# Three residual sums moved from VectorE adds into PSUM accumulation on TensorE, drained by ScalarE copies

## The reference

```
h = tok(x)                      # windowed attention: 8x8 windows, 8 heads of 8, 2D rotary, proj + proj_b
h = h + mamba(layernorm(h))     # RMS norm, in_proj, causal conv of 4 taps, silu, selective scan, out_proj,
                                #   + residual (its own normed input)
h = h + moe(layernorm(h))       # 6 experts of three layers, weights of the top 2 from a router
```

## Time and profile before

| | before |
|---|---|
| median of 3 runs | 1697.93 us (1687.25 to 1699.51) |
| profiled execution | 1679.58 us |
| its span, first to last instruction | 1677.8 us |
| PE busy | 1269.9 us (76%) |
| DVE busy | 1313.0 us (78%) |
| ACT busy | 1047.0 us (62%) |
| POOL busy | 1106.3 us (66%) |
| mean granted clock of TensorE | 0.877 |

### The profile page before, as it was taken

The page is one execution under the profiler, slowest core; times in us unless marked ns, Lnnn a source line. Parts: engine busy times, 40 slices in busy tenths (PEclk is TensorE's granted clock), DMA queues, the critical chain, the costliest instruction groups (busy, mean ns, idle before and its releaser), DMA issues. The chain is left out here.

```text
span 1677.8 us, 25769 instructions
## 1 busy us (share of the span) xinstructions
PE 1269.9 (76%) x7988; PEld 594.3 (35%) x7988; DVE 1313.0 (78%) x1719; ACT 1047.0 (62%) x1940; POOL 1106.3 (66%) x1523
## 2 busy tenths in 40 slices
PE   3675768797978778796979787887969696767565
PEld 2442515243433434252524333343425242121212
DVE  2122478898988898998989898988889798979951
ACT  2235566768677676867676777767685767474522
POOL 2013376877767686868687786868686877877740
PEclk9768988899999999898989999998999998676765
DMA  2000569686968686767767687868677687778820
GB/s 69 1 13 7 159 171 258 179 234 176 247 184 228 190 230 193 207 204 188 229 176 234 184 239 195 223 189 220 195 213 203 174 232 205 230 205 234 237 71 7
DMA packets 212961, 303.35 MB, mean 181 GB/s; under 512 B 77196, under 2 KB 77400, under 8 KB 212696
## 3 DMA queue, kind: packets, MB, share of 16 engines
q1 hardware_dynamic: 212824, 301.70, 65.0%
HBM read 274.75 MB, written 20.97 MB: 176 GB/s over the span
## 5 line engine op out<-in xcount | busy, mean ns | idle before, releaser
L1279 POOL TENSOR_TENSOR hc<-hs,c_rep 128x512 f32<-128x512 f32 x512 | 655.3, 1281 | 313.1 <-DVE hs L1062 311.1
L1062 DVE TENSOR_TENSOR_SCAN hs<-bank,state,xd 128x512 f32<-128x512 f32 x512 | 651.6, 1275 | 51.5 <-issue 36.0
L808 ACT ACTIVATE bank<-dl,a_neg 128x512 f32<-128x512 f32 x512 | 350.3, 686 | 165.4 <-DVE hs L1062 118.5
L1053 DVE TENSOR_TENSOR xd<-xd,bank 128x512 f32<-128x512 f32 x512 | 336.5, 662 | 27.6 <-DMA xd<-xdel_rows 22.4
L548 PE MATMUL bank<-q_diag,k_heads 128*128 128x128 f32 x1024 | 189.9, 308 | 10.1 <-ACT shift L801 10.1
L548 PEld LDWEIGHTS bank<-q_diag,k_heads 128*128 128x128 f32 x1024 | 167.1, 198 | 83.1 <-issue 77.5
L538 PE MATMUL bank<-k_heads,q_diag 128*128 128x512 f32 x256 | 160.5, 712 | 40.5 <-ACT pv L801 19.9
L816 ACT ACTIVATE probsT<-bank 128x512 f32<-128x512 f32 x128 | 76.4, 597 | 174.9 <-PE bank L549 174.9
L457 PE MATMUL bank<-hc,wts 128*32 128x512 f32 x1024 | 175.4, 744 | 5.2 <-POOL hc L1279 5.2
L1080 DVE TENSOR_REDUCE neg_max<-bank 128x8 f32<-128x512 f32 x128 | 87.9, 687 | 99.7 <-PE bank L538 99.0
L739 PE MATMUL bank<-e,wts 64*64 64x512 f32 x368 | 63.5, 764 | 78.8 <-ACT e L986 78.8
(11 more groups left out here) (162 smaller groups left out, 2207.0 us busy)
## 6 DMA issues: line engine op xcount, KB each, us to landing
xd<-xdel_rows SPq DMA_DIRECT2D x512, 256.0 KB, 4.5
dl<-delta_rows SPq DMA_DIRECT2D x512, 256.0 KB, 4.1
delta_rows<-delta SPq DMA_DIRECT2D x16, 512.0 KB, 7.6
xdel_rows<-xdel SPq DMA_DIRECT2D x16, 512.0 KB, 5.7
xin<-in_x_dram SPq DMA_DIRECT2D x32, 128.0 KB, 2.6
q_diag<-rot SPq DMA_DIRECT2D x32, 128.0 KB, 2.8
out_dram<-res SPq DMA_DIRECT2D x256, 16.0 KB
k_heads<-rot SPq DMA_DIRECT2D x104, 16.0 KB
```

What stands on the lines that cost most here:

```text
L808: act.activation(decay_ps[n % 2][:, :], dl[:, n % 4, :], ACT.Exp, scale=a_neg[:, g:g + 1])\
L1053: dve.tensor_tensor(xd[:, n % 8, :], xd[:, n % 8, :], b_ps[:, :], ALU.mult).then_inc(injected.sem, 1)
L1062: dve.tensor_tensor_scan(hs[:, n % 4, :], decay_ps[n % 2][:, :], xd[:, n % 8, :], state[:, u:u + 1], ALU.mult, ALU.add).then_inc(scanned.s ...
L1279: pool.tensor_tensor(hc[:, n % 8, :], hs[:, n % 4, :], c_rep[:, BAND * h:BAND * h + BAND], ALU.mult)\
```

## The change

Each sum is now made in PSUM. PE first multiplies the second summand by the identity (a 128x128 stationary `ident`, 512 moving columns, `start=True`), and the products that were there follow with `start=False`, so they accumulate on it. For "out" the four transposes become four plain products with the identity as the moving operand, as they too must accumulate. The three DVE adds are gone. ACT copies each finished bank to SBUF (hid, h1, res) and signals `drained`: hid in `normalize` n = 8, h1 in `experts` n = 5, res in `experts` n = 35. The reduces on DVE stay where they were. The call of `experts` for chunk c-2 leaves DVE's body, as nothing is left in it.

```diff
@@ tensor
                 if s == 31:
                     use = A["proj"]
                     fill(use, k)
+                    pe.matmul(use.bank[:, :], ident, h_bias[:, :].unsqueeze(1).to_broadcast([128, NW, C]),
+                              start=True, stop=True)
                     pe.wait_ge(A["oT"].drained, A["oT"].empty(k))
                     for i in range(4):
                         last = pe.matmul(use.bank[:, 128 * i:128 * i + 128], attT[:, 128 * i:128 * i + 128], col("wp"),
-                                         start=True, stop=True)
+                                         start=False, stop=True, skip_group_check=True)
...
                 if n == 4:
                     use = F["mo"]
                     fill(use, k)
+
+                    pe.wait_ge(ln1_pool.sem, ln1_pool.at(k, 15))
+                    pe.matmul(use.bank[:, :], ident, h_ln[:, q, :, :], start=True, stop=True)
                     pe.wait_ge(gated.sem, gated.at(k, 2))
                     for w in range(NW):
                         last = pe.matmul(use.bank[:, C * w:C * w + C], y_gated[:, w, :, :], col("w_out"),
-                                         start=True, stop=True)
+                                         start=False, stop=True, skip_group_check=True)
...
                 if n == SLOTS + 2:
                     use = F["out"]
                     fill(use, k)
+                    pe.matmul(use.bank[:, :], ident, h1[:, :, :], start=True, stop=True)
                     for i in range(4):
-                        last = pe.transpose(use.bank[:, 128 * i:128 * i + 128], outT[:, 128 * i:128 * i + 128], ident)
+                        last = pe.matmul(use.bank[:, 128 * i:128 * i + 128], outT[:, 128 * i:128 * i + 128], ident,
+                                         start=False, stop=True, skip_group_check=True)
@@ scalar
             def normalize(k, n):
+                if n == 8:
+                    use = A["proj"]
+                    act.wait_ge(use.filled, use.full(k))
+                    if past(k - 1):
+                        act.wait_ge(ln1_pool.sem, ln1_pool.at(k - 1, 15))
+                    copy(hid[:, :, :], use.bank[:, :].rearrange("p (w h) -> p w h", w=NW)).then_inc(use.drained, 1)
...
             def experts(k, n):
+                if n == 5:
+                    use = F["mo"]
+                    act.wait_ge(use.filled, use.full(k))
+                    copy(h1[:, :, :], use.bank[:, :].rearrange("p (w h) -> p w h", w=NW)).then_inc(use.drained, 1)
+                if n == SLOTS + 3:
+                    use = F["out"]
+                    act.wait_ge(use.filled, use.full(k))
+                    if past(k - 1):
+                        act.wait_ge(stored.sem, stored.at(k - 1, 256))
+                    copy(res[:, :, :], use.bank[:, :].rearrange("p (w h) -> p w h", w=NW)).then_inc(use.drained, 1)
@@ vector
-                if n == 8:
-                    use = A["proj"]
...
-                    dve.tensor_tensor(hid[:, :, :], use.bank[:, :].rearrange("p (w h) -> p w h", w=NW),
-                                      h_bias[:, :].unsqueeze(1).to_broadcast([128, NW, C]), ALU.add)\
...
-                    dve.tensor_tensor(h1[:, :, :], use.bank[:, :].rearrange("p (w h) -> p w h", w=NW), h_ln[:, q, :, :], ALU.add)\
-                       .then_inc(use.drained, 1)
                     dve.wait_ge(F["mo"].drained, F["mo"].empty(k))
                     dve.tensor_reduce(st[:, 0, :], h1[:, :, :], X_AXIS, ALU.add).then_inc(done.sem, 1)
...
-                    dve.tensor_tensor(res[:, :, :], use.bank[:, :].rearrange("p (w h) -> p w h", w=NW), h1[:, :, :],
-                                      ALU.add).then_inc(use.drained, 1)
```

More of the change, by code:

```diff
@@ L611, in second, with experts @@
                     from_x(k, q, "c1", "wc", 1)
-            def experts(k, n):
+            def experts(k, q, n):
                 if n == 4:
@@ L766, in body @@
                     if has(c - 2):
-                        experts(c - 2, SLOTS + n)
+                        experts(c - 2, odd, SLOTS + n)
                     if has(c - 1) and n == 1:
@@ L774, in body @@
                     if has(c - 1):
-                        experts(c - 1, n)
+                        experts(c - 1, 1 - odd, n)
                     if has(c + 1):
@@ L1111, in normalize @@
                 st, done = st_a, ln1_dve
-                if n == 8:
-                    use = A["proj"]
-                    dve.wait_ge(use.filled, use.full(k))
-                    if past(k - 1):
-                        dve.wait_ge(ln1_pool.sem, ln1_pool.at(k - 1, 15))
-                    dve.tensor_tensor(hid[:, :, :], use.bank[:, :].rearrange("p (w h) -> p w h", w=NW),
-                                      h_bias[:, :].unsqueeze(1).to_broadcast([128, NW, C]), ALU.add)\
-                       .then_inc(use.drained, 1)
                 if n == 9:
@@ L1133, in prepare, with experts @@
                     dve.tensor_scalar(xdel[:, :], ex_d[:, :], 1.0, -1.0, ALU.add, ALU.add).then_inc(soft_dve.sem, 1)
-            def experts(k, q, n):
+            def experts(k, n):
                 st, done = st_f, ln2_dve
                 if n == 5:
-                    use = F["mo"]
-                    dve.wait_ge(use.filled, use.full(k))
-                    dve.wait_ge(ln1_pool.sem, ln1_pool.at(k, 15))
-                    dve.tensor_tensor(h1[:, :, :], use.bank[:, :].rearrange("p (w h) -> p w h", w=NW), h_ln[:, q, :, :], ALU.add)\
-                       .then_inc(use.drained, 1)
                     dve.wait_ge(F["mo"].drained, F["mo"].empty(k))
@@ L1211, in body @@
                         gated_out(c, odd, 0)
-                    if has(c - 2):
-                        experts(c - 2, odd, SLOTS + n)
                     if has(c + 1):
@@ L1220, in body @@
                     if has(c - 1):
-                        experts(c - 1, 1 - odd, n)
+                        experts(c - 1, n)
             dve.memset(rw2_2[:, :], 0.0).then_inc(setup_dve, 1)
```

## The result

The change makes the kernel slower: 1796.0 us against 1695.2 us, the medians of four runs each, a ratio of 1.061 (95% interval 1.057 to 1.065). The forecast was 1798 us.

What follows compares the result with a forecast made beforehand. It took the chain PE, ACT, PE, ACT, not DVE's load, to pace slots 2 to 11. Twelve full passes at 7.0 us (84) plus 16 elsewhere gave +100 on the median 1697.93: 1798 us, range 1740 to 1830.

Steps and rivals of the forecast that it cites:

- the order decides, not DVE's load: Slots 2 to 11: the PE-ACT chain paces, not DVE's load; the load rival had 1668 us, chance 0.05.
- PE, slots 2 to 4: New products cost PE 1.39 us in slot 2 and 0.96 in slot 4; ACT's conv results move about 3.0 us.
- hid behind the table block: Slots 8 and 9: ACT copies hid only after table loads and Silu; DVE waits, scan 10 is 7.1 us late.
- what the hid stall leaves at the end of a pass: The wait for hid adds 2.6 us to xdel, 5.6 late in all, and later slots give nothing back.
- the clock, 1.4 us a pass in slots 9 to 12: PE's 6.3 us idle before k and q may lower the clock: 0 to 2.7 us on xdel, 1.4 taken.
- the replay: Slots 2 to 13 of pass 8 stepped through with durations as issued: xdel at 963.5 instead of 957.90, 5.6 late.
- the clock falls for longer: Rival: the 6 us gap keeps PE at 1.2 GHz into the attention slots; +116 to +136 us, chance 0.10.
- everything outside the full passes: Pass 0 3 us, pass 1 4, pass 14 3, pass 15 1.5, lead-in 2, tail 2.5: 16 us in sum.

Runs made afterwards that it cites:

- e7: The kernel before with only the sum of hid moved, ACT's copy of it placed ahead of the table loads; 1699.9 us, 1.007.
- e6: The kernel before with all of PE's added products, overwritten by those that follow, and DVE's adds kept; 1713.4 us, 1.012.
- e9: The kernel before plus the filler, one 512-column identity product on PE in slot 3 that nobody reads; 1666.8 us, 0.988.
- e4: The changed kernel with one call moved: ACT copies hid ahead of the table loads and Silu; 1754.3 us, 1.038 to the kernel before.
- e8: The changed kernel plus the filler, one 512-column identity product on PE in slot 3 that nobody reads; 1769.8 us, 1.046 to the kernel before.
- e1: The kernel before with only the sum of hid moved, as the diff has it; 1756.6 us, 1.042.
- e5: The kernel before with ACT's three copies, no DVE adds and no identity products, the second summands left out; 1783.9 us, 1.057.
- e3: The kernel before with only the sum of res (out) moved, as the diff has it; 1748.1 us, 1.038.
- e2: The kernel before with only the sum of h1 moved, as the diff has it; 1695.7 us, 1.004.
- e12: The kernel before plus the product in slot 3, with ACT's first z copy ahead of attention's copy in slot 6; 1671.7 us, 0.987.
- e10: The kernel before plus unread products on PE: one in slot 3, one at the end of slot 11, three in slot 16; 1674.6 us, 0.991.

## Why the prediction came out, step by step

**Right: the order decides, not DVE's load.** The 30 us that DVE sheds bring no gain. The Trainium skill (Perfetto Trace Analysis, Optimizing Scalar/DVE Operations) says that if DVE is saturated, offloading some work to Scalar may make sense. Here it didn't: with DVE busy for 90% of a pass, one sum moved with its copy well placed gave 1.007 (e7).

**Right: PE, slots 2 to 4.** From scan 0 the conv starts at 16.0 us in pass 9 (1099.74 - 1083.72) against 13.2 in pass 8 of before (933.58 - 920.34): 2.8 later, foretold 2.9. Scan 6 is 5.65 later (20.41 against 14.76), foretold 5.9. It is caught up to 2.5 by scan 9 (foretold 3.0). In e6's passes with the clock up scan 9 is 2.0 us later than in e9 (25.82 against 23.85 after scan 0), so most of this is PE's; the other 0.5 comes with ACT's copies.

**Right: hid behind the table block.** The copy starts as the second load ends, and scan 10 is 6.8 us later than before (33.02 against 26.21), foretold 7.1. e4 against the changed kernel shows it by one moved call. The price by the Trainium skill (ScalarE: Activation LUTs, What ACT_TABLE_LOAD costs), 2.66 us a switch, would have put hid 2.7 us later still; the rows have 1.30 us from 1110.99 to 1112.29, and 1.30 from 1114.21 to the copy, so the measurement speaks against it here.

**Mis-sized: what the hid stall leaves at the end of a pass.** xdel is 5.8 us later (43.37 after scan 0, was 37.56), as replayed; I then wrote "later slots are not touched" and let the pass carry 5.6. But the lateness changes on the way: scan 14 is 5.1 late, scan 19 is 6.2 late. In both kernels DVE then waits for a transfer of xd; before and after, pass 9:

```profile
1061.49 0.69 DVE L1053 TENSOR_TENSOR xd<-xd,bank 128x512 f32<-128x512 f32 x1 [1.22 <-DMA xd<-xdel_rows]
```

```profile
1140.70 0.69 DVE L1076 TENSOR_TENSOR xd<-xd,bank 128x512 f32<-128x512 f32 x1 [2.19 <-DMA xd<-xdel_rows]
```

SP issues it behind k_heads, which are made from POOL's rot. Timelines of SP, before, then after:

```profile
1048.04 3.02 SPq L349 DMA_DIRECT2D k_heads<-rot  x4
...
1057.45 0.60 SPq L337 DMA_DIRECT2D xd<-xdel_rows  x1
```

```profile
1127.21 3.01 SPq L349 DMA_DIRECT2D k_heads<-rot  x4
...
1136.60 0.60 SPq L337 DMA_DIRECT2D xd<-xdel_rows  x1
```

From their pass's scan 0 (1010.80 and 1083.72) these are at 37.2 and 46.7 us before, 43.5 and 52.9 after: the queue is 6.2 us late, and so are the scans once they need it. That the queue is what fixes the 6.2 is read from the rows; no run moved it alone. With the clock held in slots 2 to 8 (e8 and e9) a pass costs 6.4 us: 2.5 by scan 9 and 4.0 behind it (e1 alone has about 4 too), for which I had 2.6 for the stall and 1.4 for the clock.

**Mis-sized: the clock, 1.4 us a pass in slots 9 to 12.** It does fall to the low level in the gap, as the rows of L476 and L457 show. But I had priced the stretch as if it ran at full clock before. Over slots 10 to 13 of pass 8 of before, and of pass 9 of after, it is

```profile
946.55:959.23 12.68, 7.89 (x36) 2.28 (x29) 11.22 (x15) 11.09 (x17) 10.23 (x16) 0.81 0.71 186
```

```profile
1116.74:1127.70 10.96, 9.12 (x57) 2.31 (x50) 10.51 (x14) 7.00 (x13) 8.68 (x13) 0.87 0.54 144
```

0.81 before, 0.87 after: the low stretch only begins earlier. xdel of pass 9 is only 0.2 us later than the replay without any clock term. In e8 this stretch alternates between 10.9 us with 2.8 us at the low clock, as in pass 9, and 11.9 us with 5.0, so every second pass has 1 us more. The term is then an estimated 0.2 + 0.5 = 0.7 us on average instead of 1.4. It is contained in the 4.0, whose stall is then 3.3 rather than 2.6.

**Missed: the clock in slots 4 to 6.** The rival "the clock falls for longer" had it in the attention slots, as a consequence of the gap. It comes earlier, ahead of the gap, and one product in slot 3 removes it. It costs 3.3 us in slots 4 to 8 and 4.3 in the whole pass in passes 8, 10 and 12, and it is in the kernel before too (its passes 5, 6 and 12 take 92.0, 92.0 and 93.7 us instead of 89.8 to 91.7). The change made it more frequent: of passes 2 to 13, three have it before, six after, seven in e1, ten in e5, twelve in e3, but only three in e6 and two in e2. Why it comes in one pass and not in the next is open.

**Mis-sized: everything outside the full passes.** I had 16 us. Between e8 and e9 it is: first scan 4.9 us later (foretold 2), pass 0 9.3 (3), pass 1 4.3 (4), pass 14 3.8 (3), pass 15 -0.5 (1.5), tail 6.1 (2.5), together 28. The filler doesn't hold the clock in e8's pass 0; between the two kernels themselves pass 0 costs 2.3 and the whole sum is 24. The single traces spread here: e2 has the same program as the kernel before up to its first scan, and that comes at 202.9 us instead of 194.6. So the terms of a few us can't be told apart. For the tail I had read no row, and no run took it apart.

So 84 + 16 = 100 was 93 + 24 = 117 between the profiled executions of the two kernels, both terms too small, above all for the clock in slots 4 to 8; with the filler in both it was 77 + 28 = 105. The medians moved by 101, because the profiled execution of the kernel before (1679.58 us) lies 15.6 us under its median, while that of the changed kernel (1796.58) lies at it. Where the slower executions of the kernel before lose these 15.6 us no trace shows. The agreement to 2 us is in part luck; the mechanism isn't.

## What to carry to other kernels

Moving work from a full engine to a less busy one can pay only if the result is there by the time its readers need it. So look up what stands ahead of it in its new engine's order: here a table block of 4.5 us, and moving one call ahead of it, with the same instructions, was worth 42 us. A stall's own length says little: 4.5 us before h1 cost 0.5 us alone, since DVE could catch up, while 4.25 us before hid cost 4.0; there, by the rows, the next scans and the DMA queue were late with it. And look at the granted clock by stretch in several passes: a product that nobody reads, in an idle gap ahead of work on the path, took 1.2% off a tuned kernel.

## What the runs showed of the hardware

- The granted clock is not the same in equal passes. The same 513 products got 0.50 over 6.8 us in pass 8 and 1.00 in pass 9, and it was granted low in ten of twelve passes in e5, in all of them in e3, in none with one more product of 0.96 us in slot 3 (e8 to e12). This is for slots 2 to 8 of passes 2 to 13.
- A higher mean clock need not mean a shorter time. In e10 it rose to 0.907 from e9's 0.884, with 9.5 us a pass less at the low clock in slots 10 to 18 and 2.9 more behind scan 19, yet the time didn't fall.
- The first scan comes at 187.5 to 192.9 us in the five kernels with the filler and at 194.6 to 205.7 in the nine without.
- xdel on DVE (L1133, 128x1024, from SBUF to SBUF) took a median of 1.40 us before and 0.75 us after; the minimum is 0.69 in both. In pass 9 of before xdel starts during the second of POOL's two rot products (2.51 us together) and runs on beside the product with C, which takes 1.73 us instead of 1.27; xdel takes 1.39. In pass 9 of the changed kernel it starts during the first of them: xdel takes 0.69 us and the two 3.02. What sets which of the two gets slower wasn't tried.
